# Graph network kernel: 200,000 edges laid out on 125 partitions in runs of 1600, in place of 128 partitions in runs of 1563

## What is computed

```python
def _sage_conv(x, src, dst, Wl, bl, Wr):
    agg = jax.ops.segment_max(x[src], dst, num_segments=x.shape[0])
    agg = jnp.where(jnp.isfinite(agg), agg, 0.0)
    return agg @ Wl + bl + x @ Wr
...
h = jnp.maximum(_layernorm(x, axis=-1), 0.0)
x = x + _L0_gnn_ref(h, edge_index, ...)   # three layers of leaky_relu(_sage_conv(...), 0.01)
```

## Time and profile before

| | |
|---|---|
| runs before, median of 3 | 6213.08 us (6209.69 to 6213.9) |
| profiled execution, span | 7523.5 us |
| POOL busy | 4642.2 us, 62% of the span, 4852 instructions |
| DVE busy | 2890.1 us, 38% |
| PE busy | 750.9 us, 10% |
| the gathers of L316 | 4689, mean 958 ns |
| the scans of L556 | 4602 + 87, mean 439 ns |

### The profile page before, as it was taken

The page is one execution under the profiler, slowest core; times in us unless marked ns, Lnnn a source line. Parts: engine busy times, 40 slices in busy tenths (PEclk is TensorE's granted clock), DMA queues, the critical chain, the costliest instruction groups (busy, mean ns, idle before and its releaser), DMA issues. The chain is left out here.

```text
span 7523.5 us, 43085 instructions
## 1 busy us (share of the span) xinstructions
PE 750.9 (10%) x3385; PEld 458.9 (6%) x3385; DVE 2890.1 (38%) x9228; ACT 170.0 (2%) x425; POOL 4642.2 (62%) x4852
## 2 busy tenths in 40 slices
PE   0111111111110234300000000031310000000003
PEld 0000000000000112100000000021210000000002
DVE  4444444444444523333333333352333333333335
ACT  1000000000000000000000000000000000000000
POOL 5655655555565566666666666646666666666664
PEclk9999999999999955555555555565555555555556
DMA  3222222222222345555555555545555555555554
GB/s 104 83 85 84 85 83 83 82 85 83 82 88 81 97 153 198 189 178 182 172 185 170 171 188 170 184 152 176 185 184 187 174 167 188 175 174 183 174 175 148
DMA packets 378011, 1088.35 MB, mean 145 GB/s; under 512 B 94085, under 2 KB 146698, under 8 KB 377850
## 3 DMA queue, kind: packets, MB, share of 16 engines
q0 software_dynamic: 206720, 529.51, 25.6%
q1 hardware_dynamic: 147914, 537.81, 18.5%
q10 hardware_dynamic: 23216, 19.67, 0.9%
HBM read 554.47 MB, written 532.15 MB: 144 GB/s over the span
## 5 line engine op out<-in xcount | busy, mean ns | idle before, releaser
L316 POOL DMA_INDIRECT ring<-features,index_stage x4689 | 4491.3, 958 | 2667.4 <-issue 2193.2
L556 DVE SCALAR_TENSOR_TENSOR ring<-ring,restart 128x256 f32<-128x256 f32 (+1 forms) x4602 | 2020.2, 439 | 3006.2 <-issue 2725.7
L561 DVE TENSOR_SCALAR ring<-lane_bf,dst_lane 128x128 bf16<-128x128 bf16 x1563 | 421.6, 270 | 276.7 <-issue 259.5
L564 DVE TENSOR_SCALAR ring<-lane_bf,dst_tile 128x50 bf16<-128x50 bf16 x1563 | 398.6, 255 | 273.9 <-issue 272.3
L543 DVE COPY index_stage<-src_t 128x6 int32 x756 | 138.6, 183 | 805.9 <-issue 760.1
L773 PE MATMUL carry_ps<-ident,carry 128*128 128x128 f32 x5 | 1.8, 444 | 3664.0 <-DVE carry L570 3664.0
L745 PE MATMUL mm_ps<-ring 128*128 128x50 bf16 x1563 | 112.7, 219 | 2214.1 <-DVE ring L564 1791.4
L734 PE MATMUL mm_ps<-wr,h_turned 128*128 128x256 f32 (+1 forms) x500 | 225.7, 597 | 689.6 <-issue 497.2
L773 PEld LDWEIGHTS carry_ps<-ident,carry 128*128 128x128 f32 x5 | 0.9, 234 | 3665.0 <-DVE carry L570 3665.0
L745 PEld LDWEIGHTS mm_ps<-ring 128*128 128x128 bf16 x1563 | 77.4, 117 | 2264.1 <-DVE ring L564 1829.5
L351 POOL DMA_INDIRECT ring<-running_max_log,end_stage x150 | 144.4, 963 | 115.0 <-DVE end_stage L621 61.1
(11 more groups left out here) (91 smaller groups left out, 395.2 us busy)
## 6 DMA issues: line engine op xcount, KB each, us to landing
running_max_log<-ring SPq DMA_DIRECT2D x520, 768.0 KB
running_max_log<-ring SPq DMA_DIRECT2D x262, 384.0 KB
ring<-features,index_stage POOLq DMA_INDIRECT x4689
features<-h_out SPq DMA_DIRECT2D x50, 256.0 KB
h_in<-features ACTq DMA_DIRECT2D x100, 128.0 KB
ring<-x SPq DMA_DIRECT2D x5, 640.0 KB, 7.8
features<-ring SPq DMA_DIRECT2D x5, 640.0 KB, 4.0
h_in<-features ACTq DMA_DIRECT2D x50, 64.0 KB
```

The source lines that it names most:

```text
L316: pool.indirect_dma_start(ring[:, c * w:(c + 1) * w], None, tables[l], bass.IndirectOffsetOnAxis(ap=index_stage[:, b, u:u + 1].bitcast(U32 ...
L556: dve.scalar_tensor_tensor(out=here, in0=before, scalar=restart[:, bass.ds(i * RING_COLS + c, 1)], in1=here, op0=ALU.add, op1=ALU.max).the ...
L561: dve.tensor_scalar(hot[:, c, 0:P], lane_bf[:, :], dst_lane[:, bass.ds(i * RING_COLS + c, 1)], None, ALU.is_equal).then_inc(hot_ready, 1)
L564: dve.tensor_scalar(hot[:, c, P:HOT], lane_bf[:, 0:TILES], dst_tile[:, bass.ds(i * RING_COLS + c, 1)], None, ALU.is_equal).then_inc(hot_re ...
```

## The change

The host cuts the edge list into 1600 edges per partition (`cols = -(-edges // RUNS)`, with `RUNS` = 125). The arrays still have 128 rows; rows 125 to 127 hold only filling edges. `COLS` becomes 1600, `STEPS` 30, and the last step has 34 columns. A gather of L316 names 125 partitions. All else (scans, one-hot rows, log, the gathers at the end of a layer) keeps its 128 partitions. Because partitions 125 to 127 of `ring` are written by no gather now, DVE sets partitions 96 to 127 of the ring to zero once, after `h0_stored` and ahead of staging the first row numbers. The wait on `edges_loaded` in the scan loop is taken out.

```diff
+RUNS = 125
...
+        idle_zeroed = sem("idle_zeroed")
...
                             pool.indirect_dma_start(
-                                ring[:, c * w:(c + 1) * w], None, tables[l],
+                                ring[0:RUNS, c * w:(c + 1) * w], None, tables[l],
                                 bass.IndirectOffsetOnAxis(
-                                    ap=index_stage[:, b, u:u + 1].bitcast(U32), axis=0),
+                                    ap=index_stage[0:RUNS, b, u:u + 1].bitcast(U32), axis=0),
                             ).then_inc(landed[b], DMA)
...
+            dve.wait_ge(h0_stored, DMA * TAIL_STEPS)
+            dve.memset(ring[96:P, :], 0.0).then_inc(idle_zeroed, 1)
+
             def stage_first_step():
+                dve.wait_ge(idle_zeroed, 1)
                 for b in range(BLOCKS):
...
                         if not last:
 
-                            dve.wait_ge(edges_loaded, 3 * DMA)
                             dve.tensor_copy(
...
-    cols = -(-edges // P)
+    cols = -(-edges // RUNS)
```

## The result

The changed kernel takes 7722.5 us (median of 4 runs, 7717.1 to 7723.5), the kernel before 6213.5 us beside it. The ratio is 1.2424 with a 95% interval of 1.2406 to 1.2443: **24% slower**, 1509 us. I had forecast 6312 us. One thing is needed to read what follows: the kernel before took about 6210 us in some sets of runs and about 7500 us in others, and the trace shown ahead of the prediction (7523.5 us) is of the second kind; the changed kernel took 7722 us beside the first and 7800 us beside the second.

The account below looks back on a forecast made before the run. The prediction took POOL's slots as the bound (gathers times 1.25 us, plus about 350). It summed 6213.1 + 85.5 (gathers) + 11.5 (zeroing) + 2.5 (layer ends) = 6312.6, said as 6312 us, with range 5450 to 6560 us.

Parts of the forecast that it names:

- What bounds the kernel: Whole kernel: POOL's slots, one gather start to the next, bind the timed runs; gathers times 1.25 us, plus about 350.
- the holes: Larger idle gaps between POOL's gathers, 1231 us in the trace; the timed runs were said to hold next to none.
- The price of a gather: POOL's gathers: 4800 of 125 rows at a slot of 1.2394 us, 5949.1 us in all, +85.5 us; forecast's chance 0.40.
- the first two: Bounds of POOL's gather slot: unchanged 1.2505 us, +138.8 us; or busy part going by rows, 1.2283 us, +32.2 us.
- Rival 2: POOL's gathers: cost goes by rows of one share, 25 for 8; a tenth gives 7336 us; 0.15 with another case.
- another case: DMA transfers become the bound, one lasting about 16/5 as long with five shares; folded into Rival 2, together 0.15.
- a fiftieth: Rival 2 with a fiftieth of 0.949 us grown by 25/8: 0.040 us more per gather, 6558 us.
- Rival 1: POOL's gathers: five shares in place of sixteen make them cheaper; a tenth gives 6054 us, a quarter 5584; chance 0.40.
- The rule weighed against the trace: DMA engines per gather: the largest number up to 16 dividing the rows; 128 rows use 16, 125 five; no price given.
- Zeroing: Start: DVE zeroes 13,824 words in 11.4 us; first gather at about 48.5 in place of 37.5, +11.5 us.
- Layer ends: End of each layer: last block has four columns for three, and a longer log write, three times; +2.5 us.
- Packets: POOL's queue: count near 211,456 if sixteen shares remain, otherwise another count.

Follow-up runs that it names:

- before_paused: The kernel before with three semaphore increments on POOL behind each gather and nothing else; 6207.6 us, ratio 1.0001.
- layout_only_b: The changed kernel with 1600 columns kept but each gather naming all 128 partitions, second run; 6348.6 us, ratio 1.0231 to the kernel before.
- pause_two: The changed kernel with its edges back on 128 partitions, plus two semaphore increments on POOL after each gather; 6220.2 us, ratio 1.0021 to the kernel before.

## Why the prediction was wrong, step by step

- **What bounds the kernel: right.** I concluded from span, slots and median that the timed runs had next to none of the holes and were bound by POOL's slots. before_paused and layout_only_b show such executions, in 6207.7 and 6346.5 us of span, with waits of DVE ended by landings. What I could not know from one trace is that the holes are no matter of being profiled: in other sets of runs the timed runs of the kernel before have them too, and profiled executions have none in before_paused, pause_two and layout_only_b.
- **The price of a gather: wrong, and this is the step that failed.** "These differ by little, and nothing favours either of the first two, so I take their middle: slot 1.2394, 5949.1, +85.5 us." The slot is 1.535 on average, and the term that was put at 85.5 us is 1493 (139 for 111 more gathers, 1354 for the dearer 4800). I bounded it by rows that all name 128 partitions and by an assumption that fewer rows cannot cost more. The runs show about 0.83 us plus 13 to 15 ns for each row of a share, with 25 rows in a share in place of 8.
- **Rival 2 had the mechanism and nearly its size.** I priced "a tenth of 0.949 grown by 25/8" at 0.202 us and 7336 us. Measured: eight rows' worth is 8 x 0.0136 = 0.109 us, 11% of 0.949; seventeen more rows are 0.231, and the gather's median grew by 0.263. The 0.03 left are about what fifteen shares cost over sixteen. That the tenth was so near is luck: no row of the trace gave it. I gave the rival 0.15 together with another case and let the range reach only to a fiftieth. Rival 1, on the other side, had 0.40; nothing of it is seen: 5 shares are not cheaper than 16.
- **The rule weighed against the trace.** The split of 125 rows over five engines stood in the prediction, filed under "no price". It should have widened the slot's bounds instead: by it a share has 25 rows and not 8, a shape that no row of the trace shows, and rows of gathers with shares of 8 cannot bound its price.
- **Zeroing: right in kind, small in size.** 11.58 us against 11.4, but 15.1 at the first gather against 11.5 (the start said, 48.5 for 37.5, is 11.0), since DVE needed 3 us to start after the store and POOL one more after the copy.
- **Layer ends:** layout_only_b is 142 us over the kernel before, and 139 for 111 gathers and 14 for the start are 153 already. The 2.5 us cannot be seen.
- **Packets:** that the count stays near 211,456 with sixteen shares and is another one otherwise was the right thing to look at: it was 544,256.

## What to carry to other kernels

Price an indirect DMA on POOL by rows per share: divide the number of partitions by its largest divisor up to sixteen. Here 128, 64 and 16 partitions make sixteen shares, 125 only five, 127 one; on POOL a gather of three rows fewer cost 28% more, one of one row fewer 170% more. And where an engine's queue bounds the time, a shape that the trace has never shown needs a run before it is believed, and a wide range until then.

## What the runs showed of the hardware that I had not expected

- A gather of 16 rows costs POOL 0.847 us and one of 128 rows 0.949 us: nearly all is fixed. Idle engines get as many packets as busy ones, with 4 B for each row: 112 packets a gather on average with 125 rows, 43 with 128.
- The kernel before differs by 21% between sets of runs (6206 to 6213 and 7498 to 7519 us), and both kinds occurred under one chip number, while the changed kernel, with slower gathers, differs by 1%. Where it is slow, DVE issues its scans late (2796 us of waits ended by "issue" in the trace before), and POOL has holes; that POOL then waits for room in the ring is named by the profile for 432.6 us and an inference for the rest. With three semaphore increments behind each gather the time was 3% under that of the kernel before. What delays DVE there is open.
